# VectorE writes both biases into the residual's place, and the DMA that brings x adds x to them

## The reference, cut to what matters

```python
# conditional 1x1 mixing: attention over 8 kernels, per batch
att   = softmax(mlp(cond_128))                     # (128, 8)
agg_w = einsum('bk,koi->boi', att, weight)         # (128, 64, 64)
agg_b = att @ bias_k                               # (128, 64): one number per row of y
y     = einsum('boi,bih->boh', agg_w, x) + agg_b[:, :, None]
# feed-forward with 8 low-rank experts, the best 2 per row
combine  = top-2 of softmax(y @ W_router.T), renormalised
h        = einsum('nd,erd->ner', y, A) * combine
expert   = einsum('ner,eor->no', h, B) * 2
out      = x + y @ W_base.T + b_base + expert
```

## Time and profile before

| | |
|---|---|
| time, median of 3 runs | 1030.17 us (1029.88 to 1030.34) |
| the profiled execution's own time | 1032.57 us |
| its span, first to last instruction | 1030.6 us |
| TensorE busy | 963.7 us, 94% |
| VectorE busy | 830.4 us, 81% |
| ScalarE busy | 399.7 us, 39% |
| GpSimd busy | 437.9 us, 42% |
| mean granted TensorE clock | 0.988 of full speed |
| DMA | 112.45 MB, mean 109 GB/s |

### The profile page before, as it was taken

How to read it: one execution, slowest core, us unless ns; L and a number is a source line. 1 busy time by engine, 2 the same in 40 slices (tenths; PEclk the granted TensorE clock), 3 DMA queues, 4 the chain that set the end, 5 groups by cost and what they waited for, 6 DMA issues and landing times.

```text
span 1030.6 us, 19700 instructions
## 1 busy us (share of the span) xinstructions
PE 963.7 (94%) x6697; PEld 941.9 (91%) x6697; DVE 830.4 (81%) x1496; ACT 399.7 (39%) x791; POOL 437.9 (42%) x326
## 2 busy tenths in 40 slices
PE   6869999999999999999999999999999999999996
PEld 5869999999999999999999999999999999999995
DVE  4888888887887888887788888788888888878873
ACT  4443344334234334334433423433433343343341
POOL 0143444443443544344444444354534445443452
PEclk9989999999999999999999999999999999999998
DMA  5523322223322123332222332222333222233312
GB/s 201 198 99 126 117 91 87 101 103 125 125 104 103 64 104 124 125 125 90 90 90 103 125 125 106 102 69 116 107 125 125 103 89 78 103 125 125 117 50 81
DMA packets 35084, 112.45 MB, mean 109 GB/s; under 512 B 13024, under 2 KB 13280, under 8 KB 30464
## 3 DMA queue, kind: packets, MB, share of 16 engines
q1 hardware_dynamic: 35072, 112.29, 30.2%
HBM read 76.56 MB, written 35.65 MB: 109 GB/s over the span
## 4 chain that ended last, share of the span: by engine, by line
PE 77%; DVE 14%; issue 4%; ACT 3%; DMA 1%; DVEq 0%; ACTq 0%
PE ps L384 19%; PE ps L382 19%; PE ps L386 19%; PE ps L430 9%; DVE x_lo L786 6%; PE ps L407 4%; PE ps L408 3%; PE ps L409 3%; DVE sum L805 2%; DVE z_lo L814 2%; ACT z_hi L591 2%; DVE w_lo L876 1%; PE ps L443 1%; DMA w_stage<-in_wide 1%; ACT w_hi L603 1%
## 5 line engine op out<-in xcount | busy, mean ns | idle before, releaser
L382 PE MATMUL ps<-w_hi,x_hi 128*128 128x290 f32 x1792 | 540.5, 302 | 11.8 <-DVE w_lo L876 7.6
L384 PE MATMUL ps<-w_lo,x_hi 128*128 128x290 f32 x1792 | 535.7, 299 | 0.0
L386 PE MATMUL ps<-w_hi,x_lo 128*128 128x290 f32 x1792 | 533.7, 298 | 0.0
L382 PEld LDWEIGHTS ps<-w_hi,x_hi 128*128 128x128 f32 x1792 | 341.0, 190 | 15.4 <-issue 11.9
L386 PEld LDWEIGHTS ps<-w_hi,x_lo 128*128 128x128 f32 x1792 | 341.3, 190 | 0.0
L384 PEld LDWEIGHTS ps<-w_lo,x_hi 128*128 128x128 f32 x1792 | 341.1, 190 | 0.0
L765 POOL TENSOR_TENSOR x_sb<-x_sb,row_bias 128x512 f32<-128x512 f32 x128 | 201.4, 1573 | 272.3 <-ACT row_bias L571 272.3
L760 POOL TENSOR_TENSOR x_sb<-x_sb,bias_out 128x512 f32<-128x512 f32 x128 | 193.4, 1531 | 191.0 <-DMA x_sb<-in_x 191.0
L786 DVE TENSOR_TENSOR x_lo<-xT_sb,x_hi 128x512 fp32r<-128x512 f32 x192 | 206.8, 1079 | 56.4 <-ACT x_hi L559 56.4
L559 ACT CAST x_hi<-xT_sb 128x512 fp32r<-128x512 f32 x192 | 118.6, 619 | 246.1 <-DVE xT_sb L802 211.3
L407 PE MATMUL ps<-z_hi,mix_hi 128*128 128x388 f32 (+1 forms) x192 | 69.0, 359 | 38.1 <-DVE z_lo L814 36.5
(11 more groups left out here) (85 smaller groups left out, 970.2 us busy)
## 6 DMA issues: line engine op xcount, KB each, us to landing
x_sb<-in_x SPq DMA_DIRECT2D x64, 512.0 KB, 4.5
result<-x_sb SPq DMA_DIRECT2D x64, 512.0 KB, 2.7
xT_sb<-in_xT SPq DMA_DIRECT2D x31, 1024.0 KB, 4.8
w_stage<-in_wide SPq DMA_DIRECT2D x3, 1160.0 KB, 6.7
agg_w_rows<-agg_w SPq DMA_DIRECT2D x1, 2048.0 KB, 8.7
mix<-agg_w_rows SPq DMA_DIRECT2D x124, 16.0 KB, 2.2
w_stage<-in_wide SPq DMA_DIRECT2D x2, 580.0 KB, 7.4
b_stage<-in_wide SPq DMA_DIRECT2D x1, 1160.0 KB, 13.6
```

What stands on the lines that cost most here:

```text
L382: nc.tensor.matmul(dst, x_hi[:, s, rows], w_hi[:, w, c, cols], start=first, stop=False, skip_group_check=True)
L384: nc.tensor.matmul(dst, x_hi[:, s, rows], w_lo[:, w, c, cols], start=False, stop=False, skip_group_check=True)
L386: mm = nc.tensor.matmul(dst, x_lo[:, s, rows], w_hi[:, w, c, cols], start=False, stop=last, skip_group_check=True)
```

## The change

GpSimd's four additions per unit and side and ScalarE's `bias_of` go, and with them `row_bias` and the loads of x on SyncE's queue. VectorE gets one instruction per tile, `put_biases`, that writes col_sum * agg_b + bias_out over the whole place of the residual (128 x 1024), when the result before it has been stored. GpSimd then issues a DMA per tile that reads x from memory and adds it to what stands in the place (`accum_op=ALU.add`). `result` waits for that DMA.

```diff
 # SyncE
-            def load_x(u, side):
-                sp.dma_start(x_sb[:, side, :], x_tiles[tile_no(u, side)]).then_inc(x_in[side], 16)
...
-                sp.wait_ge(stored[0], u * 16)
-                load_x(u, 0)
                 store(u - 1, 1)
                 if not last:
                     sp.wait_ge(mix_lo_done, tile_no(u, 1) + 1)
                     load_mix(u + 1, 1)
-                sp.wait_ge(stored[1], u * 16)
-                load_x(u, 1)
 # ScalarE: every bias_of and wait_row_bias_free goes
-                nc.scalar.mul(row_bias[:], col_sum[:, cols], agg_b[:, bass.ds(tile_no(u, side), 1)]
-                              ).then_inc(row_bias_done, 1)
 # GpSimd
-            def add_biases(u, side):
-...
+            def add_x(u, side):
+
                 t = tile_no(u, side)
+                pool.wait_ge(biased, t + 1)
+                pool.dma_start(x_sb[:, side, :], x_tiles[t], accum_op=ALU.add).then_inc(x_in[side], 16)
...
             def unit(u, par, last):
                 mix_low(u, 0)
-                add_biases(u - 1, 1)
                 mix_low(u, 1)
-                add_biases(u, 0)
+                add_x(u, 0)
+                add_x(u, 1)
 # VectorE
             def result(u, side):
                 t = tile_no(u, side)
-                dve.wait_ge(x_biased, t * 2 + 2)
+                dve.wait_ge(x_in[side], u * 16 + 16)
...
+            def put_biases(u, side):
+
+                nc.vector.scalar_tensor_tensor(x_sb[:, side, :], col_sum[:, AR:WIDE],
+                                               agg_b[:, bass.ds(tile_no(u, side), 1)], bias_out[:], ALU.mult, ALU.add
+                                               ).then_inc(biased, 1)
...
             # ahead of the units
+            dve.wait_ge(bias_out_in, 16)
+            dve.wait_ge(agg_w_out, 16)
+            put_biases(0, 0)
+            put_biases(0, 1)
...
                 hwT_low(u - 1, 1)
+                dve.wait_ge(stored[0], u * 16)
                 z11_low(u)
+                put_biases(u, 0)
                 dve.wait_ge(p5_saved, u + 1)
                 dve.wait_ge(product_mm, count(u, "S3"))
                 add_acc(sum3, a, z22_summed)
                 result(u - 1, 1)
...
                 if not last:
                     x_low(u + 1, "A12")
                     dve.wait_ge(x_lo_done, count(u + 1, "A11"))
+                    dve.wait_ge(stored[1], u * 16)
                     make_s2(u + 1)
+                else:
+                    dve.wait_ge(stored[1], u * 16)
+                put_biases(u, 1)
```

More of the change, by code:

```diff
@@ L36 @@
 ROUTE_STEPS = 9
-DH = D // 2
 B11, B21, T1, B22, T2, T3, T4 = range(7)
@@ L159, in build @@
         bias_out = sb("bias_out", [P, D])
-        row_bias = sb("row_bias", [P, DH])
         ar = sb("ar", [P, AR])
@@ L209, in build @@
         x_lo_done = sem("x_lo_done")
-        x_based = sem("x_based")
-        x_biased = sem("x_biased")
-        row_bias_done = sem("row_bias_done")
+        biased = sem("biased")
         mix_hi_done = sem("mix_hi_done")
@@ L341, in _ @@
             sp.wait_ge(agg_w_out, 16)
-            load_x(0, 0)
-            load_x(0, 1)
             sp.wait_ge(mix_lo_done, 2)
@@ L676, in _ @@
             act.wait_ge(col_sum_done, 2)
-            bias_of(0, 0, 0)
             act.wait_ge(bT_in, 16)
@@ L683, in _ @@
             x_high("A12")
-            wait_row_bias_free(0, 0, 1)
-            bias_of(0, 0, 1)
             def unit(u, par, last):
@@ L694, in unit @@
                 gate(u - 1, 0)
-                wait_row_bias_free(u - 1, 1, 0)
                 mix_high(u, 0)
-                bias_of(u - 1, 1, 0)
                 act.wait_ge(product_mm, count(u, "A11"))
@@ L703, in unit @@
                 act.wait_ge(product_mm, count(u, "A12"))
-                wait_row_bias_free(u - 1, 1, 1)
                 x_high("S4")
-                bias_of(u - 1, 1, 1)
                 act.wait_ge(product_mm, count(u, "S2"))
@@ L715, in unit @@
                 hwT_high(u - 1, 1)
-                wait_row_bias_free(u, 0, 0)
                 z11_high(u)
-                bias_of(u, 0, 0)
                 if not last:
@@ L722, in unit @@
                     x_high("A11")
[L723 to L727, removed]
+                z12_high(u)
+                if not last:
                     act.wait_ge(product_mm, count(u, "S4"))
-                    wait_row_bias_free(u, 0, 1)
                     x_high("A12")
-                bias_of(u, 0, 1)
             units(act, unit)
@@ L737, in _ @@
             hwT_high(LAST, 0)
[L738 to L741, removed]
             gate(LAST, 1)
@@ L753, in mix_low @@
                                         ALU.subtract).then_inc(mix_lo_done, 1)
-            def add_biases(u, side):
+            def add_x(u, side):
                 t = tile_no(u, side)
[L757 to L766, removed]
+                pool.wait_ge(biased, t + 1)
+                pool.dma_start(x_sb[:, side, :], x_tiles[t], accum_op=ALU.add).then_inc(x_in[side], 16)
             for side in range(2):
                 mix_low(0, side)
-            pool.wait_ge(bias_out_in, 16)
-            add_biases(0, 0)
+            add_x(0, 0)
+            add_x(0, 1)
             def unit(u, par, last):
                 mix_low(u, 0)
-                add_biases(u - 1, 1)
                 mix_low(u, 1)
-                add_biases(u, 0)
+                add_x(u, 0)
+                add_x(u, 1)
             units(pool, unit)
-            add_biases(LAST, 1)
         @block.vector
```

## The result

The changed kernel takes 979.92 us (median of 4 runs, 979.49 to 980.81), the kernel before 1030.03 us (4 runs, 1028.03 to 1030.34) on the same chip: ratio 0.9519, 95% interval 0.9502 to 0.9535. A later repeat gave 979.91 us and 0.9518 (0.9504 to 0.9532). The prediction said 981, with 975 to 1000. The profiled execution took 979.68 us with a span of 978.0 us.

The account below looks back on a forecast made before the run. TensorE was taken as the bound, waiting in each unit for VectorE's z12, which GpSimd's additions delayed. Savings of 43.5 + 2.9 + 3.3 = 49.7 us from 1030.2 gave 980.5, say 981 us, range 975 to 1000.

Parts of the forecast that it names:

- The cause: On VectorE ahead of z12: GpSimd's additions stretch `make_s1`, `make_s3` and `x_low`; at 0.68 us each VectorE gains 2.61 us.
- 30 x 1.45 + 2.9 = 46.4 us in the units: TensorE's 30 waits for z12, 1.45 us each, go, and 2.9 us of the experts' waits for `hwT_low`.
- The start, 3.3 us: Before the units: last weight's low part 0.9 us, the `x_low` ahead 1.1 us and the weight's load 1.3 us sooner.
- The sum, 49.7 us: Whole kernel: 43.5 us of z12 waits, 2.9 us of experts' waits and 3.3 us at the start are saved.
- `put_biases` at 1.27 us, hidden: On VectorE, once per tile: 1.27 us, priced between 1217 ns and 1.69 us, hidden from TensorE on both sides.
- 0.8 to 0.9 us to spare ahead of z12, 0.6 and 1.0 on side 1: Slack after the change: before TensorE needs z12; VectorE's idle left before `z21_low`; and between `hw` and its transpose.
- rival (a): The z12 wait shrinks but stays because VectorE doesn't reach 0.68 us: 1002 us with half left, 991 with a quarter; chance 0.19.
- The store of side 1, 3.0 us: VectorE's wait for `stored[1]` ahead of `make_s2`: the store takes 3.0 us against some 4.6 us of work, spare 1.6 us.
- Rival (b): Side 1's store lands late beside side 0's accumulating DMA; TensorE loses above 6.2 us, 1066 us at 9 us; chance 0.06.
- The accumulating DMA, 4 to 7 us to landing: GpSimd's DMA adding x lands in 4 to 7 us, hidden, needed by `result` 18.8 to 20 us later.
- (c): GpSimd isn't what stretches VectorE; `put_biases` only adds 0.34 us per unit ahead of z12: 1040 us; chance 0.03.
- (d): The z12 gain comes, but TensorE meets another wait of similar size, ending within 2 us of before; chance 0.02.

Follow-up runs that it names:

- e3: The kernel before without GpSimd's bias additions and ScalarE's `row_bias` products, loads of x still on SyncE's queue: 979.21 us.
- e9: The changed kernel with four GpSimd additions of 128x512 into a spare buffer behind side 0's DMA issue only: 1057.52 us.
- e13: The changed kernel with one GpSimd memset of 128x1024 per unit behind side 0's DMA issue, beside `make_s1`: 980.81 us.
- e10: The changed kernel with GpSimd's DMA of x as a plain load without accumulation, so both biases are missing: 979.55 us.
- e7: The changed kernel with two more 512-column instructions like `put_biases` on VectorE, into a spare buffer, behind `put_biases` of side 0: 1000.43 us.
- e8: The changed kernel with two more 512-column instructions like `put_biases` on VectorE, into a spare buffer, behind `put_biases` of side 1: 1002.20 us.
- e6: The changed kernel with four GpSimd additions of 128x512 into a spare buffer behind side 1's DMA issue only: 1144.20 us.
- e5: The changed kernel with four GpSimd additions of 128x512 into a spare buffer behind each of its DMA issues, both sides: 1214.77 us.
- e4: The changed kernel with GpSimd waiting for the store of side 1 before it issues side 0's accumulating DMA: 978.97 us.
- e12: The changed kernel with GpSimd waiting for side 1's store before side 0's DMA, run again beside the unchanged changed kernel: 979.22 us.

## Why the prediction was right

**The cause.** Right, and shown from both sides: without the additions the three instructions take 0.68 to 0.69 us (after, e3), with additions at the old place 1.56, 1.61 and 1.77 us (e9). Its wording, that the two are slow when they "are in SBUF together", was too wide: a GpSimd that writes there holds nothing (e13). The prediction had the place from the earlier trace rows and the proof of contrast from `make_s4` at 0.678 us.

**30 x 1.45 + 2.9 = 46.4 us in the units.** Measured 47.8. The term was a little small: 1.45 was worked out from one unit, while the list of waits held 46.0 / 30 = 1.53 us of weight load; the slow second unit took 1.1 back: 46.0 + 2.9 - 1.1 = 47.8. The experts' wait for `hwT_low` is gone from the list, as said.

**The start, 3.3 us.** Measured 4.0. The wait for the last weight went from 7.25 us to 3.81 and its matmul started 2.96 us earlier (63.50 to 60.54). Of its terms the last split (3.49 to 2.57 us) and the `x_low` (1.77 to 0.68) came as said, and the weight's load gave 0.8 us (6.71 to 5.90) in place of 1.3. What was left out is `z11_low` (1.16 to 0.75 us), and that TensorE's stretch at 1.2 GHz got shorter too: its granted clock is 0.50 until about 68.6 us before, 5.1 us of matmuls, and until about 63.3 after, 2.8 us, which is the other 1.0. Other executions of the kernel after and of its near variants are at the place of 73.38 between 72.9 and 73.9, so the 4.0 is good to half a us.

**The sum, 49.7 us.** The medians differ by 50.1 us. The spans of the profiled executions differ by 52.6: the terms were 2.9 us small in all, and the profiled execution of before was itself 2.4 us above its median. The close agreement of 981 with 979.9 is partly these two cancelling.

**`put_biases` at 1.27 us, hidden.** Measured 1278 ns. The lower end of the range (the plain subtraction, 1217 ns) was the near one, the upper (1.69 us, from small forms) was wrong, in part since L855's 400 ns held stretched executions, as the prediction warned: the same instruction has 368 ns after, and 1.17 ns per column from there gives 1.42. Hidden on both sides, as e3 and e10 show.

**0.8 to 0.9 us to spare ahead of z12, 0.6 and 1.0 on side 1.** Right in size. Measured ahead of z12: 0.9 to the matmul in the timeline, 0.73 in e7. On side 1 the 0.6 us of idle time before `z21_low` is gone, used by the wait for the store, and of the rest 0.8 us is left in the timeline (`hw` ends at 503.25, the transpose starts at 504.07), 0.73 in e8. The slack, and not the busy shares, is what made rival (a) fail.

**The store of side 1, 3.0 us.** The step that was mis-sized: 5.4 us in the unit shown, 7.1 in the first. The prediction had named a wait of VectorE for `stored` as a sign of being wrong, and there are 27.2 us of it; the forecast stood all the same, since the slack behind hid it. Rival (b), with a chance of 0.06, had the mechanism exactly (the accumulating DMA of side 0 on its way when the store is issued) and its limit of 6.2 us holds: 5.4 plus the 0.73 left is 6.1, and the unit with 7.05 is the one that lost 1.1. It deserved more than 0.06; the kernel stands 0.7 us from losing.

**The accumulating DMA, 4 to 7 us to landing.** Measured 5.3, from 5.1 to 7.4 us, and it is needed some 19 us later; the 64 issues take 862 to 1013 ns. The stall of GpSimd's descriptors of which the Trainium skill warns ("SBUF — State Buffer", the section on its two separate sides) did not show. But the page ties that stall to VectorE's 2-port modes and says that `tensor_tensor` has none, so the prediction took the warning wider than it is given, and these runs hardly test it.

**Rivals (c) and (d)** are dead: e9 and e3 for (c), a period of 28.77 us with no TensorE wait in it for (d).

## What to carry to other kernels

Before work goes from VectorE to GpSimd, look at which VectorE instructions beside it read two tensors from SBUF: each waits until the GpSimd instruction that reads SBUF beside it has ended, so many small ones beside long additions are the worst case (`route` in e6: 164 us), and work that only writes held nothing here (e13). A VectorE instruction of 1.28 us in a place with slack was cheaper than four GpSimd additions "off the critical path" that stretched three instructions on it. Work that goes to a DMA should be placed by what else that DMA delays: here a store, 0.7 us short of mattering.

## What the runs showed of the hardware that was not expected

- The holding doesn't scale with the held instruction: 128x1 from 0.16 to 1.63 us, 128x512 from 0.68 to 1.56 to 1.77 us, beside additions of 1.3 to 1.6 us each (e5, e9). Forms with one of their two tensors in PSUM are not held (`z21_low` 0.76 us).
- GpSimd is held as well: in the kernel before, `make_s2` takes its 0.69 us at 495.39, and the addition that began at 495.36 takes 1.86, where three of e5 between small instructions take 1.26 to 1.28. The means are 1354 ns in e6, beside `route`, and 1610 in e9, beside the three large ones.
- A DMA of 512 KB that accumulates lands in 5.3 us where the plain one takes 3.7 (e10), and no sooner when the store has landed first (5.4, e4 and e12); a store issued 1.4 us behind it takes 5.4 us instead of 2.7 to 3; beside the plain one it passes.
- With a wait of 2.3 us in each unit (e9), TensorE ran at 1.2 GHz for some 3 us behind the wait in one unit of five, at 1.5 us more each; beside the waits of up to 7 us in e5 and e6 its busy time grew by 84 and 48 us.
